# An expert layer computed transposed, with its weights copied by VectorE, in a GNN and mixture-of-experts kernel

## The chip, the cores and the metric

The kernel runs on one core of a Trainium2 chip. A core has TensorE (matmuls, its clock granted at 1.2 or 2.4 GHz), VectorE, ScalarE, GpSimd, and SyncE, which here only starts DMAs. Each runs its own program and they meet by semaphores. The metric is the device time of one execution in microseconds, as a median of runs; the lines below come from one profiled execution.

## The reference

There are 6250 nodes with 256 features and 100,000 edges. A GNN layer comes first (messages over the edges, sums per node, an update of the nodes); then each node is a token of a mixture of eight experts, each token going to its two best:

```python
x = x + gnn(layernorm(x), edges, ...)          # messages and node update
t = layernorm(x)
probs = softmax(t @ router_w.T); rw, re = top_k(probs, 2); rw = rw / rw.sum(-1)
out = t
for e in range(8):
    h = gelu(t @ w1[e] + b1[e])                # 256 -> 256
    out = out + combine[:, e:e+1] * (h @ w2[e] + b2[e])
x = x + out
```

All of the part treated here is float32.

## The kernel before, in words

The program is a row of blocks, each ended by a barrier of all engines: sorting of the edges, messages (the longest, from about 530 to 2112 us), node update, routing tables, and the expert block, in which the change lies.

The node update takes the 50 blocks of 125 nodes in 25 pairs. SyncE loads `x` for it (L1403), stores zeros into the slots of the routed token arrays (L1391) and loads the expert weights on the side (L1407), among them the biases `b1` and `b2`, each broadcast over 128 partitions. Before the first pair, two transposes by TensorE and one ScalarE copy turn `router_w` (L1537, L1491).

The routing block computes with VectorE the experts, the gates and each token's slot, and writes a table that says which expert each tile of 128 slots belongs to. SyncE sends the table to DRAM and back into one row (`tabrow`, L1647, L1649), and waits for it to land before the block ends. The engines load their registers from that row.

In the expert block tokens are first routed. `route(i)` on VectorE makes for node block t of choice k the normalized rows (L1849, `tensor_scalar`) and the slot's id and gate (L1850) in a ring `ts` of four buffers; GpSimd scatters them to `xsd[k]` by an indirect DMA (L1814). For the first choice ScalarE adds the base row, what the output starts from (L1914). All 50 first-choice blocks are routed before the experts start; the 50 of the second choice are spread over the first expert steps by `beside(m)`: four in each step below LY, two in each after.

Then 56 pairs of tiles (128 tokens each) run through a software pipeline: 28 first-choice pairs, then 28 second-choice pairs. In step m each engine does its part for pair m minus a lag; with names and lags of before:

- SyncE loads the pair (L1798, eight buffers deep) and, for first-choice pairs, the base rows (L1802). The load into a reused buffer waits for the row ids of eight pairs earlier (`slot_row`).
- TensorE, in this order: transposes the tokens of pair m (L1957), layer one of pair m-2 (L1967), layer two of pair m-6 (L1978), transposes the hidden rows of pair m-4 (L1988). A float32 matmul shows as two instructions, each with its own weight load. In layer one the tokens are the stationary operand and the expert's 256 columns, at an address from a register, stream past.
- VectorE, in this order: the routed rows; bias of layer one, pair m-2 (L1878); output of pair m-6: bias (L1887), then gate times it plus the base row (L1893) in the first half, gate alone (L1896) in the second; row ids and gates of pair m-1 (L1904, L1905).
- ScalarE: copy of the transposed tokens of pair m-1 (L1922), Gelu of pair m-3 (L1927), copy of the transposed hidden rows of pair m-5 (L1932).
- GpSimd: the scatters of the routed rows, and for pair m-7 two scatters of output rows into `out` (L1824): plain writes in the first half, accumulating in the second.

Semaphores hold these together: for instance TensorE's layer one of pair a waits until the bias of pair a-2 has freed its bank (`hb_ready`), and VectorE's output of pair a until the scatters of pair a-4 have landed (`y_out`).

Of the kernel before, what the change touches and what calls it, by code (L numbers as in the profile page):

```python
# [21 lines left out]
P = 128  # L22
N, D, E, X = 6250, 256, 100000, 8
KC = D // P
# [117 lines left out]
def gnn_moe_kernel(nc, x, src, dst, edge_w, mW1, mb1, ln_g, ln_b, mW2, mb2, uW1, ub1, uW2, ub2,  # L142
                   router_w, w1, b1, w2, b2, out):
    ctx = ExitStack()
    with ctx:
# [1149 lines left out]
        rwr = wcut(D)  # L1295
        ub1T = wcut(KC)
# [58 lines left out]
        rwT_ready = sem("rwT_ready")  # L1355
        tb_ready = sem("tb_ready")
# [11 lines left out]
        with nc.Block() as block:  # L1368
            @block.sync
            def _(sp):  # L1370
                sp.dma_start(uW1s, uW1[D:2 * D, :].rearrange("(k p) n -> p k n", p=P)).then_inc(uw_in, 16)
                sp.dma_start(uW2s, uW2.rearrange("(k p) n -> p k n", p=P)).then_inc(uw_in, 16)
                sp.dma_start(ub1T, ub1.rearrange("(k p) -> p k", p=P)).then_inc(uw_in, 16)
                sp.dma_start(rwr[0:X], router_w).then_inc(uw_in, 16)
                expert_weights = [(w1s[:, 0], w1[:, 0:P, :].rearrange("e p n -> p e n")),
                                  (w1s[:, 1], w1[:, P:2 * P, :].rearrange("e p n -> p e n")),
                                  (w2s[:, 0], w2[:, 0:P, :].rearrange("e p n -> p e n")),
                                  (w2s[:, 1], w2[:, P:2 * P, :].rearrange("e p n -> p e n")),
                                  (b1b, b1.rearrange("e n -> (e n)").partition_broadcast(P)),
                                  (b2b, b2.rearrange("e n -> (e n)").partition_broadcast(P))]  # L1380
                WAT = 2

                sp.wait_ge(padrow_set, 2)
                sp.dma_start(out[N:N + XD * P, :].rearrange("(d p) f -> p d f", p=P), padrow[:, :, 0:D]).then_inc(xpads_out, 16)
                UNITS = XC // (XD // 2)

                def empty_slots(n):

                    k, g, wide = (1, n * (XD // 2), XW) if n < UNITS else (0, (n - UNITS) * (XD // 2), XB)
                    slots = xsd[k][g * P:(g + XD // 2) * P, :].rearrange("(g p) f -> p g f", p=P)  # L1390
                    sp.dma_start(slots, padrow[:, g % XD:g % XD + XD // 2, 0:wide]).then_inc(xpads_out, 16)  # L1391

                def step(m):
                    a = m - UA
                    if a.within(NP2):
                        wait(sp, y1b_ready, a.of(1, -1))
                        sp.dma_start(un[a.mod(2)], ud[bass.ds(a.of(), 1)].rearrange("t p k u n -> (t p) k (u n)")).then_inc(un_in[a.mod(2)], 16)
                    s = m.mod(RP)
                    if m.within(NP2):
                        wait(sp, xh_ready, m.of(1, 1 - RP))  # L1400
                        rows = x[bass.ds(m.of(2 * NB), 2 * NB), :].rearrange("(u p) f -> p u f", p=NB)
                        for p in PARTS:
                            sp.dma_start(xp[s][p], rows[p]).then_inc(xp_in[s], 16)  # L1403
                        empty_slots(m.c)
                    if isinstance(m.it, int) and WAT <= m.c < WAT + len(expert_weights):
                        into, rows = expert_weights[m.c - WAT]
                        sp.dma_start(into, rows).then_inc(fw_in, 16)  # L1407
                for m in range(NP2 + UA):
                    step(Step(0, RP, m))
                for n in range(NP2, 2 * UNITS):  # L1410
                    empty_slots(n)
                sp.wait_ge(fw_in, 16 * (2 * KC + 2))
                sp.wait_ge(xpads_out, 16 * (2 * UNITS + 1))
# [74 lines left out]
            def _(act):  # L1488
                act.wait_ge(uw_in, 64)
                act.wait_ge(rw_tr, 1)  # L1490
                nc.scalar.activation(rws, ps[:, 7, 0:KC * X].rearrange("p (k e) -> p k e", k=KC), ACT.Copy).then_inc(rwT_ready, 1)  # L1491

# [40 lines left out]
            def _(pe):  # L1533
                t_ = nc.tensor
                pe.wait_ge(uw_in, 64)
                for k in range(KC):
                    last = t_.transpose(ps[:, 7, k * X:(k + 1) * X], rwr[0:X, k * P:(k + 1) * P], ident[0:X, 0:X])  # L1537
# [85 lines left out]
        with nc.Block() as block:  # L1623
# [20 lines left out]
            def _(sp):  # L1644
# [6 lines left out]
                sp.wait_ge(xtab_in, 16)  # L1651
# [92 lines left out]
        RB = 2  # L1744
        LXT, L1, LG1, L2H, LHT, L2 = 1, 2, 3, 4, 5, 6
# [10 lines left out]
        hg = cut(RH * 2 * D, "p (r u n) -> p r u n", r=RH, u=2)  # L1756
        hT = cut(RH * 2 * D, "p (r n) -> p r n", r=RH)
        hb = work[:, WORK - 2 * 2 * D:WORK].rearrange("p (r u n) -> p r u n", r=2, u=2)
# [6 lines left out]
        base_ready = sem("base_ready")  # L1765
# [4 lines left out]
        slot_row = sem("slot_row")  # L1770
        h_ps = sem("h_ps")
        hb_ready = sem("hb_ready")
        hg_ready = sem("hg_ready")
        h_tr = sem("h_tr")
# [11 lines left out]
        with nc.Block() as block:  # L1786
# [18 lines left out]
            def _(pool):  # L1805
# [3 lines left out]
                def route(i):  # L1809
                    k, t = divmod(i, BK)  # L1810
                    pool.wait_ge(ts_ready, i + 1)
                    if k == 0:
                        pool.wait_ge(base_ready, t + 1)
# [27 lines left out]
            def _(dve):  # L1841
                v = nc.vector

                def route(i):
# [4 lines left out]
                    v.tensor_scalar(ts[n_, r, 0:D], agg[n_, t, :], mv3[n_, t:t + 1, 1], mv3[n_, t:t + 1, 0], ALU.mult, ALU.add)  # L1849
# [5 lines left out]

                regs = [v.alloc_register(f"expert_of_tile{j}") for j in range(2 * (RX + L2))]
# [9 lines left out]
                for m in range(XP + L2):  # L1866
# [5 lines left out]
                    a = m - L1  # L1872
                    if 0 <= a < XP:
                        dve.wait_ge(h_ps, a + 1)
                        wait(dve, hg_ready, a - 1)
                        for u in range(2):
                            o = offs[2 * (b + L2 - L1) + u]
                            last = v.tensor_tensor(hb[:, a % 2, u], ps[:, 2 + a % 2, u * D:(u + 1) * D], b1b[:, bass.ds(o, D)], ALU.add)  # L1878
                        last.then_inc(hb_ready, 1)
                    a = m - L2  # L1880
                    if 0 <= a < XP:
# [3 lines left out]
                        for u in range(2):  # L1885
                            o = offs[2 * b + u]
                            v.tensor_tensor(yb[:, r, u], ps[:, 6 + a % 2, u * D:(u + 1) * D], b2b[:, bass.ds(o, D)], ALU.add).then_inc(y_raw, 1)  # L1887
# [11 lines left out]
                    if 0 <= a < XP:  # L1899
                        r = a % RX  # L1900
# [7 lines left out]
            def _(act):  # L1908
                act.wait_ge(ts_spare, 1)
                for t in range(BK):  # L1910
                    r = t % RS
                    if t >= RS:
                        act.wait_ge(ts_out[r], 16 * (t // RS))
                    nc.scalar.activation(ts[n_, r, XW:XB], agg[n_, t, :], ACT.Identity, bias=mv3[n_, t:t + 1, 0],  # L1914
                                         scale=xscale[n_, t:t + 1]).then_inc(base_ready, 1)

                def step(m):
                    a = m - LXT
# [5 lines left out]
                    if a.within(XP):  # L1924
                        act.wait_ge(hb_ready, a.of(1, 1))
                        wait(act, h_tr, a.of(1, 1 - RH))
                        nc.scalar.activation(hg[:, a.mod(RH)], hb[:, a.mod(2)], ACT.Gelu).then_inc(hg_ready, 1)  # L1927
                    a = m - LHT
                    if a.within(XP):
                        act.wait_ge(h_tr, a.of(1, 1))  # L1930
                        wait(act, y_ps, a.of(1, 1 - RH))
                        nc.scalar.activation(hT[:, a.mod(RH)], ps[:, 4 + a.mod(2), :], ACT.Copy).then_inc(hT_ready, 1)  # L1932
                pipeline(act, XP, L2, RX, step)

            @block.tensor
            def _(pe):
                t_ = nc.tensor
                regs = [t_.alloc_register(f"expert_of_tile{j}") for j in range(2 * (RX + L2))]
# [9 lines left out]
                def step(m):  # L1948
# [11 lines left out]
                    if a.within(XP):  # L1960
                        pe.wait_ge(xsT_ready, a.of(1, 1))
                        wait(pe, hb_ready, a.of(1, -1))
                        for u in range(2):
                            o = offs[2 * (b + L2 - L1) + u]
                            for k in range(KC):
                                c = (u * KC + k) * P
                                last = t_.matmul(ps[:, 2 + a.mod(2), u * D:(u + 1) * D], xsT[:, a.mod(RH), c:c + P], w1f[:, k, bass.ds(o, D)],  # L1967
                                                 start=(k == 0), stop=(k == KC - 1))
                        last.then_inc(h_ps, 1)
                    a = m - L2  # L1970
                    if a.within(XP):
                        pe.wait_ge(hT_ready, a.of(1, 1))
                        wait(pe, yb_ready, a.of(1, -1))
                        for u in range(2):
                            o = offs[2 * b + u]
                            for k in range(KC):
                                c = (u * KC + k) * P
                                last = t_.matmul(ps[:, 6 + a.mod(2), u * D:(u + 1) * D], hT[:, a.mod(RH), c:c + P], w2f[:, k, bass.ds(o, D)],  # L1978
                                                 start=(k == 0), stop=(k == KC - 1))
                        last.then_inc(y_ps, 1)  # L1980
                    a = m - L2H
                    if a.within(XP):
                        pe.wait_ge(hg_ready, a.of(1, 1))
                        wait(pe, hT_ready, a.of(1, -1))
                        for u in range(2):
                            for k in range(KC):
                                c = (u * KC + k) * P
                                last = t_.transpose(ps[:, 4 + a.mod(2), c:c + P], hg[:, a.mod(RH), u, k * P:(k + 1) * P], ident[:, :])  # L1988
                        last.then_inc(h_tr, 1)
# [22 lines left out]
```

## Time and profile before

| what | value |
|---|---|
| median of 3 runs | 2656.83 us (2654.34 to 2657.34) |
| the profiled execution's own time | 2656.25 us |
| its span, first to last instruction | 2654.4 us |
| mean granted TensorE clock | 0.949 of full |
| TensorE busy (matmuls) | 2380.0 us, 90% |
| VectorE busy | 2007.8 us, 76% |
| ScalarE busy | 1716.5 us, 65% |
| GpSimd busy | 1353.1 us, 51% |

The busy times are sums over stages with different limits. Times in the views are microseconds from the first instruction; the expert block runs from about 2301 us to the end, its first expert step begins at 2372.29. In a timeline row the number after the start is how long the merged instructions took from the first start to the last end, `x8` their count, and the brackets give the engine's idle time before and what ended it.

### The profile page before, as it was taken

To read this page: it belongs to the slowest core of one execution; us is meant where nothing else is said; L and a number is where in the kernel's file an instruction comes from. 1 tells how busy PE (TensorE), PEld (TensorE's weight loads), DVE (VectorE), ACT (ScalarE), POOL (GpSimd) and SP (SyncE) were. 2 spreads that over 40 slices of the span, in tenths; PEclk is the share of its full clock that TensorE was granted. 3 is DMA by queue.
4 is the path that set the end of the run, shared out by engine and by line. 5 is a ranking of instruction groups with operands and counts; after the bars stand their busy time and mean duration, and the time that the engine had idled before them with its cause. 6 is when DMAs were issued, how large, how long until landed. Compare 5 with 4: busy or idle time off the path is not lost. (4 is left out here: it accounts for less than half of the span.)

```text
span 2654.4 us, 61287 instructions
## 1 busy us (share of the span) xinstructions
PE 2380.0 (90%) x15214; PEld 2044.3 (77%) x15215; DVE 2007.8 (76%) x6154; ACT 1716.5 (65%) x5986; POOL 1353.1 (51%) x1342
## 2 busy tenths in 40 slices
PE   4399999789999999999999999999999889119997
PEld 4288887568888888888888888888888779117886
DVE  8999999477777777777777777777777656546653
ACT  1777777567777777777777777777777556233432
POOL 2067777465555555555555555555555101267666
PEclk7599999989999999999999999999999989559998
DMA  7011111243232323232322332323235299156675
GB/s 151 1 34 29 34 34 29 86 114 91 87 92 87 91 87 91 87 91 87 91 87 89 89 91 87 91 87 91 87 91 86 62 289 307 67 204 203 208 123 65
DMA packets 155377, 265.16 MB, mean 100 GB/s; under 512 B 31249, under 2 KB 99440, under 8 KB 154917
## 3 DMA queue, kind: packets, MB, share of 16 engines
q0 software_dynamic: 64656, 147.39, 21.2%
q1 hardware_dynamic: 90623, 116.59, 14.6%
q8 instruction: 46, 0.75, 0.1%
q14 instruction: 52, 0.43, 0.1%
HBM read 190.85 MB, written 73.02 MB: 99 GB/s over the span
## 5 line engine op out<-in xcount | busy, mean ns | idle before, releaser
L1056 POOL DMA_INDIRECT work<-dst_half,stage_i x848 | 811.6, 957 | 758.3 <-PE ps L1264 582.5
L1247 PE MATMUL ps<-W2c,work 128*128 128x256 f32 x3392 | 802.3, 379 | 0.0
L1247 PEld LDWEIGHTS ps<-W2c,work 128*128 128x128 f32 x3392 | 612.0, 190 | 70.7
L1082 DVE TENSOR_TENSOR agg<-agg,ps 125x256 f32 x848 | 354.2, 418 | 254.0 <-PE ps L1264 246.3
L1188 ACT ACTIVATE work<-ps 128x512 f32<-128x512 f32 x424 | 251.9, 594 | 351.5 <-PE ps L1264 351.4
L1264 PE MATMUL ps<-work 128*125 128x256 f32 x1696 | 435.2, 379 | 1.3 <-ACT work L1209 1.3
L1203 ACT ACTIVATE work<-work 128x256 f32<-128x256 f32 x848 | 341.4, 404 | 53.6 <-DVE work L1109 50.1
L1161 DVE SCALAR_TENSOR_TENSOR work<-ps,work,b2c 128x256 f32<-128x256 f32 x848 | 368.4, 476 | 0.0
L1238 PE MATMUL ps<-ablk,work 128*128 x2544 | 351.1, 275 | 16.3 <-DVE work L1130 10.4
L519 POOL DMA_INDIRECT edge_records<-stage,work x208 | 262.6, 1263 | 176.2 <-PE ps L946 113.2
L1195 ACT ACTIVATE work<-work 128x256 f32<-128x256 f32 x848 | 340.8, 406 | 0.3
L1238 PEld LDWEIGHTS ps<-ablk,work 128*128 128x128 bf16 x2544 | 250.3, 98 | 100.4 <-issue 19.2
L1264 PEld LDWEIGHTS ps<-work 128*125 128x125 f32 x1696 | 285.4, 188 | 25.8 <-ACT work L1209 1.7
L1153 DVE TENSOR_TENSOR work<-ps,work 128x512 f32<-128x512 f32 x424 | 289.7, 683 | 0.0
L1209 ACT ACTIVATE work<-work 128x512 f32<-128x512 f32 x424 | 265.0, 625 | 10.7 <-DVE work L1161 10.7
L1257 PE MATMUL ps<-ident,work 128*128 128x128 f32 x1696 | 255.3, 273 | 0.0
L1257 PEld LDWEIGHTS ps<-ident,work 128*128 128x128 f32 x1696 | 212.7, 141 | 42.6
L812 ACT ACTIVATE work<-work 125x52 f32<-125x52 bf16 x800 | 191.1, 327 | 42.7 <-DVE work L659 38.3
L946 PEld LDWEIGHTS ps<-work 125*128 125x128 f32 x1600 | 191.2, 195 | 32.8 <-issue 15.5
L946 PE MATMUL ps<-work 125*128 125x104 f32 x1600 | 195.5, 278 | 20.6 <-ACT work L812 18.8
L1824 POOL DMA_INDIRECT out<-work x112 | 141.6, 1264 | 64.6 <-DVE work L1896 22.0
L1172 DVE TENSOR_TENSOR work<-iota_f,rec 128x250 f32<-128x250 f32 x424 | 174.3, 411 | 0.0
(280 smaller groups left out, 3366.8 us busy)
## 6 DMA issues: line engine op xcount, KB each, us to landing
work<-tile_sources SPq DMA_DIRECT2D x106, 250.0 KB
first_choice_tokens<-work SPq DMA_DIRECT2D x14, 1028.0 KB
work<-dst_half,stage_i POOLq DMA_INDIRECT x848, 2.8
second_choice_tokens<-work SPq DMA_DIRECT2D x14, 516.0 KB
work<-first_choice_tokens SPq DMA_DIRECT2D x28, 258.0 KB, 3.7
work<-second_choice_tokens SPq DMA_DIRECT2D x28, 258.0 KB, 2.9
work<-first_choice_tokens SPq DMA_DIRECT2D x28, 256.0 KB, 3.4
update_node_half<-work SPq DMA_DIRECT2D x25, 250.0 KB, 2.2
```

The source lines that it names most:

```text
L946: last = t_.matmul(ps[:, 5, 0:2 * LO], hi1[e, r, c, :], lov[e, r, c].rearrange("p f n -> p (f n)"), start=(s + c == 0), stop=(s * SB + c = ...
L1056: pool.indirect_dma_start(bg[:, r, u, :], None, dstd, bass.IndirectOffsetOnAxis(ap=stage_i[:, c:c + 1], axis=0)).then_inc(gath[r], 16)
L1082: v.tensor_tensor(d, d, ps[0:NB, (7, 0)[a.mod(2)], u * D:(u + 1) * D], ALU.add).then_inc(agg_add, 1)
L1153: v.tensor_tensor(bg[:, r].rearrange("p u n -> p (u n)"), ps[:, 1 + s, :], bg[:, r].rearrange("p u n -> p (u n)"), ALU.add).then_inc(pre_s ...
L1161: last = v.scalar_tensor_tensor(out=zb[:, u], in0=ps[:, 5 + s, u * D:(u + 1) * D], scalar=rstd[:, z.mod(RQ), u:u + 1], in1=b2c[:, :], op0= ...
L1195: last = nc.scalar.activation(junk[:, u], sa[:, a.mod(RS), u], ACT.Square, accum_out=ssq[:, a.mod(RQ), u:u + 1])
L1203: last = nc.scalar.activation(sa[:, a.mod(RS), u], bg[:, a.mod(RB), u], ACT.Silu, accum_out=ssum[:, a.mod(RQ), u:u + 1])
L1209: nc.scalar.activation(msg[:, a.mod(2)], zb[:, :, :], ACT.Silu).then_inc(msg_ready, 1)
L1238: last = t_.matmul(ps[:, 1 + s, u * D:(u + 1) * D], ohT[:, m.mod(8) // TB, c:c + P], ablkf[:, bass.ds(o + k * D, D)], start=(k == 0), stop ...
L1247: last = t_.matmul(ps[:, 5 + s, u * D:(u + 1) * D], sT[:, a.mod(RT), u, k], W2c[:, k], start=(k == 0), stop=(k == KC - 1))
L1257: last = t_.transpose(ps[:, 3 + s, c:c + P], sa[:, a.mod(RS), u, k * P:(k + 1) * P], ident[:, :])
L1264: last = t_.matmul(ps[0:NB, (7, 0)[a.mod(2)], u * D:(u + 1) * D], eh[:, a.mod(RE), u], msg[:, a.mod(2), u], start=True, stop=True)
```

## The change

Layer one is computed transposed: the expert's weights become the stationary operand (128 x 128 blocks) and the transposed tokens stream past, 128 columns at a time, so that the hidden rows come out already transposed. The second set of transposes and their copy go, with `hb`, `hg` and their semaphores. The bias of layer one now lies along the partitions, so ScalarE's Gelu adds it, in four instructions of 128 columns for each pair in place of one of 512; for this `b1` is loaded as eight rows, turned by two more transposes of TensorE, and copied into `b1b` by ScalarE. VectorE copies each tile's expert weights, 512 floats in each partition, from the register's address into one of two buffers (`w1p`), in its step for pair m-1, ahead of the row ids and behind the output of pair m-4. The lags become L1 = 2, LG1 = 3, L2 = 4, LY = 5; layer two has four PSUM banks. The normalized rows of the second choice are made by ScalarE (`act_part`), at the start of its expert steps; VectorE keeps the id and gate copy. SyncE no longer waits for the table's landing in the routing block; the engines that read it wait when they first need it.

```diff
+                sp.dma_start(b1r[0:X], b1).then_inc(uw_in, 16)
-                                  (b1b, b1.rearrange("e n -> (e n)").partition_broadcast(P)),
...
-                act.wait_ge(uw_in, 64)
+                act.wait_ge(uw_in, 80)
+                nc.scalar.activation(b1b.rearrange("p (e n) -> p e n", e=X)[:, :, 0:KC],
+                                     ps[:, 7, KC * X:2 * KC * X].rearrange("p (k e) -> p e k", k=KC), ACT.Copy).then_inc(b1T_ready, 1)
...
+                for k in range(KC):
+                    last = t_.transpose(ps[:, 7, (KC + k) * X:(KC + k + 1) * X], b1r[0:X, k * P:(k + 1) * P], ident[0:X, 0:X])
...
-                sp.wait_ge(xtab_in, 16)
...
-        LXT, L1, LG1, L2H, LHT, L2 = 1, 2, 3, 4, 5, 6
+        LXT, L1, LG1, L2 = 1, 2, 3, 4
...
@@ VectorE, route(i) @@
+                    if k == 0:
+                        v.tensor_scalar(ts[n_, r, 0:D], agg[n_, t, :], mv3[n_, t:t + 1, 1], mv3[n_, t:t + 1, 0], ALU.mult, ALU.add)
...
@@ VectorE, step m: the bias of layer one is gone; behind the output of pair m - L2: @@
                     a = m - LXT
                     if 0 <= a < XP:
+                        wait(dve, h_ps, a - RW + 1)
+                        for u in range(2):
+                            o = offs[2 * (b + L2 - LXT) + u]
+                            v.tensor_copy(w1p[:, a % RW, u], w1f[:, :, bass.ds(o, D)]).then_inc(w1p_ready, 1)
...
@@ ScalarE @@
+                def act_part(i):
+                    k, t = divmod(i, BK)
+                    r = i % RS
+                    if i >= RS:
+                        act.wait_ge(ts_out[r], 16 * (i // RS))
+                    row, scale = ((ts[n_, r, XW:XB], xscale[n_, t:t + 1]), (ts[n_, r, 0:D], mv3[n_, t:t + 1, 1]))[k]
+                    nc.scalar.activation(row, agg[n_, t, :], ACT.Identity, bias=mv3[n_, t:t + 1, 0],
+                                         scale=scale).then_inc(act_row, 1)
...
+                        act.wait_ge(h_ps, a.of(1, 1))
                         wait(act, y_ps, a.of(1, 1 - RH))
+                        for u in range(2):
+                            o = offs[2 * b + u]
+                            for f in range(KC):
+                                c = (u * KC + f) * P
+                                last = nc.scalar.activation(hT[:, a.mod(RH), c:c + P], ps[:, 2 + a.mod(2), c:c + P], ACT.Gelu,
+                                                            bias=b1b[:, bass.ds(o + f, 1)])
...
@@ TensorE, step m @@
                     a = m - L1
                     if a.within(XP):
                         pe.wait_ge(xsT_ready, a.of(1, 1))
+                        wait(pe, hT_ready, a.of(1, -1))
+                        pe.wait_ge(w1p_ready, a.of(2, 2))
+                        for u in range(2):
+                            for f in range(KC):
+                                for k in range(KC):
+                                    last = t_.matmul(ps[:, 2 + a.mod(2), (u * KC + f) * P:(u * KC + f + 1) * P],
+                                                     w1p[:, a.mod(RW), u, k, f * P:(f + 1) * P], xsT[:, a.mod(RH), (u * KC + k) * P:(u * KC + k + 1) * P],
+                                                     start=(k == 0), stop=(k == KC - 1))
                         last.then_inc(h_ps, 1)
                     a = m - L2
                     if a.within(XP):
                         pe.wait_ge(hT_ready, a.of(1, 1))
-                        wait(pe, yb_ready, a.of(1, -1))
+                        wait(pe, yb_ready, a.of(1, 1 - RH))
-                    a = m - L2H
```

## Rows read from the trace of the kernel before

**Rows 1.** Windows: us; PE, PEld, DVE, ACT, POOL busy; PEclk; DMA share; GB/s.
```profile
2540.00:2590.00 50.00, 50.00 (x280) 44.69 (x280) 25.51 (x94) 20.27 (x36) 35.61 (x24) 1.00 0.79 121
```

**Rows 2.** The chain that ended last, from 2200 us: start, us, what.
```profile
2376.21 0.96 POOL second_choice_tokens L1814
...
2563.16 1.73 PE ps L1967 x8
...
2642.91 1.55 POOL out L1824
2644.77 1.55 POOL out L1824
```

**Rows 3.** Timeline of all engines, one step of the second half: start, us, instruction.
```profile
2560.40 1.89 PE L1978 MATMUL ps<-ablk,work 128*128 x8
...
2562.43 0.76 DVE L1887 TENSOR_TENSOR work<-ps,ablk 128x256 f32<-128x256 f32 x2 [0.97 <-PE ps L1978]
...
2562.56 0.60 PE L1957 MATMUL ps<-ident,work 128*128 128x128 f32 x4
...
2563.00 1.89 PE L1967 MATMUL ps<-ablk,work 128*128 x8
2563.11 0.61 DVE L1896 TENSOR_SCALAR work<-work 128x256 f32<-128x256 f32 x2
...
2563.63 0.16 DVE L1904 CAST work<-work 128x2 int32<-128x2 f32 x1
...
2564.73 1.89 PE L1978 MATMUL ps<-ablk,work 128*128 x8
```

**Rows 4.** VectorE's timeline, first-choice steps.
```profile
2386.12 0.75 DVE L1878 TENSOR_TENSOR work<-ps,ablk 128x256 f32<-128x256 f32 x2
...
2398.65 0.41 DVE L1849 TENSOR_SCALAR work<-agg,ablk 125x256 f32<-125x256 f32 x1 [1.42 <-DMA second_choice_tokens<-work,rec]
...
2409.14 0.74 DVE L1887 TENSOR_TENSOR work<-ps,ablk 128x256 f32<-128x256 f32 x2
2409.81 0.86 DVE L1893 SCALAR_TENSOR_TENSOR work<-work 128x256 f32<-128x256 f32 x2
2410.60 0.16 DVE L1904 CAST work<-work 128x2 int32<-128x2 f32 x1
```

**Rows 5.** TensorE's timeline, an early expert step after a long wait.
```profile
2387.11 3.56 PE L1967 MATMUL ps<-ablk,work 128*128 x8 [6.76 <-DVE work L1878]
```

**Rows 6.** TensorE's timeline where 125-column float matmuls run, and a gap.
```profile
489.42 1.05 PE L920 MATMUL ps<-agg,work 128*128 128x125 f32 x8
490.32 1.88 PE L927 MATMUL ps<-work,agg 128*125 128x512 f32 x4
...
500.32 1.13 PE L965 MATMUL ps<-work 128*128 128x256 f32 x4 [2.12 <-DVE work L730]
```

**Rows 7.** Groups of VectorE over the whole span: count, busy us, mean ns, idle before.
```profile
L1694 DVE COPY work<-ablk 125x400 f32<-125x400 f32 x2 | 1.0, 520 | 0.1
...
L568 DVE COPY work<-work 125x800 f32<-125x800 f32 x1 | 0.7, 650 | 0.0
```

**Rows 8.** A group of ScalarE, the same columns.
```profile
L1914 ACT ACTIVATE work<-agg,ablk 125x256 f32<-125x256 f32 x50 | 29.7, 600 | 60.2 <-DMA first_choice_tokens<-work,rec 32.1 <-POOL work L1807 28.0
```

**Rows 9.** SyncE's line 1802 (base rows): issues and landing.
```profile
DMA to landing us min/median/max: 2.7/3.4/4.6
```

**Rows 10.** SyncE's waits, 2280 to 2302 us: us in total, times, longest.
```profile
SPq L1623 <- DMA work<-tile_experts: 3.0, 1, 3.0
```

**Rows 11.** Waits, 2110 to 2172 us.
```profile
DVE work L1481 <- DMA work<-in_x: 27.9, 9, 7.9
```

**Rows 12.** DMA, 2110 to 2170 us: packets, MB, mean rate.
```profile
DMA packets 15532, 17.91 MB, mean 298 GB/s; under 512 B 1023, under 2 KB 15272, under 8 KB 15272
```

**Rows 13.** TensorE's timeline, update stage, around one gap.
```profile
2164.43 1.39 PE L1545 MATMUL ps<-ident,work 125*128 125x125 f32 x8 [1.69 <-ACT work L1509]
2165.62 3.29 PE L1560 MATMUL ps<-ablk,work 128*125 128x256 f32 x8
```

More of the change, by code:

```diff
@@ L1295, in gnn_moe_kernel @@
         rwr = wcut(D)
+        b1r = wcut(D)
         ub1T = wcut(KC)
@@ L1355, in gnn_moe_kernel @@
         rwT_ready = sem("rwT_ready")
+        b1T_ready = sem("b1T_ready")
         tb_ready = sem("tb_ready")
@@ L1411, in _ @@
                     empty_slots(n)
-                sp.wait_ge(fw_in, 16 * (2 * KC + 2))
+                sp.wait_ge(fw_in, 16 * (2 * KC + 1))
                 sp.wait_ge(xpads_out, 16 * (2 * UNITS + 1))
@@ L1534, in _ @@
                 t_ = nc.tensor
-                pe.wait_ge(uw_in, 64)
+                pe.wait_ge(uw_in, 80)
                 for k in range(KC):
-                    last = t_.transpose(ps[:, 7, k * X:(k + 1) * X], rwr[0:X, k * P:(k + 1) * P], ident[0:X, 0:X])
+                    t_.transpose(ps[:, 7, k * X:(k + 1) * X], rwr[0:X, k * P:(k + 1) * P], ident[0:X, 0:X])
+                for k in range(KC):
+                    last = t_.transpose(ps[:, 7, (KC + k) * X:(KC + k + 1) * X], b1r[0:X, k * P:(k + 1) * P], ident[0:X, 0:X])
                 last.then_inc(rw_tr, 1)
@@ L1743, in gnn_moe_kernel @@
         RX, RY, RS, RH = 8, 4, 4, 4
-        RB = 2
-        LXT, L1, LG1, L2H, LHT, L2 = 1, 2, 3, 4, 5, 6
+        RB, RW = 2, 2
+        LXT, L1, LG1, L2 = 1, 2, 3, 4
         LY = L2 + 1
@@ L1755, in gnn_moe_kernel @@
         xsT = cut(RH * 2 * D, "p (r n) -> p r n", r=RH)
-        hg = cut(RH * 2 * D, "p (r u n) -> p r u n", r=RH, u=2)
         hT = cut(RH * 2 * D, "p (r n) -> p r n", r=RH)
-        hb = work[:, WORK - 2 * 2 * D:WORK].rearrange("p (r u n) -> p r u n", r=2, u=2)
+        w1p = cut(RW * 2 * KC * D, "p (r u k n) -> p r u k n", r=RW, u=2, k=KC)
         w1f = w1s.rearrange("p k e n -> p k (e n)")
@@ L1764, in gnn_moe_kernel @@
         ts_out = [sem(f"ts_out{r}") for r in range(RS)]
-        base_ready = sem("base_ready")
+        act_row = sem("act_row")
         base_in = [sem(f"base_in{r}") for r in range(RB)]
@@ L1770, in gnn_moe_kernel @@
         slot_row = sem("slot_row")
+        w1p_ready = sem("pair_weights")
         h_ps = sem("h_ps")
-        hb_ready = sem("hb_ready")
-        hg_ready = sem("hg_ready")
-        h_tr = sem("h_tr")
         hT_ready = sem("hT_ready")
@@ L1811, in route @@
                     pool.wait_ge(ts_ready, i + 1)
-                    if k == 0:
-                        pool.wait_ge(base_ready, t + 1)
+                    pool.wait_ge(act_row, i + 1)
                     pool.indirect_dma_start(xsd[k], bass.IndirectOffsetOnAxis(ap=xposi[:, k, t:t + 1], axis=0),
@@ L1848, in route @@
                         dve.wait_ge(ts_out[r], 16 * (i // RS))
-                    v.tensor_scalar(ts[n_, r, 0:D], agg[n_, t, :], mv3[n_, t:t + 1, 1], mv3[n_, t:t + 1, 0], ALU.mult, ALU.add)
+                    if k == 0:
+                        v.tensor_scalar(ts[n_, r, 0:D], agg[n_, t, :], mv3[n_, t:t + 1, 1], mv3[n_, t:t + 1, 0], ALU.mult, ALU.add)
                     v.tensor_copy(ts[n_, r, D:XW], idgate[n_, k, t, :]).then_inc(ts_ready, 1)
@@ L1854, in _ @@
                     route(t)
+                dve.wait_ge(xtab_in, 16)
                 regs = [v.alloc_register(f"expert_of_tile{j}") for j in range(2 * (RX + L2))]
@@ L1871, in _ @@
                         route(i)
[L1872 to L1879, printed above, removed]
                     a = m - L2
@@ L1886, in _ @@
                             o = offs[2 * b + u]
-                            v.tensor_tensor(yb[:, r, u], ps[:, 6 + a % 2, u * D:(u + 1) * D], b2b[:, bass.ds(o, D)], ALU.add).then_inc(y_raw, 1)
+                            v.tensor_tensor(yb[:, r, u], ps[:, 4 + a % RH, u * D:(u + 1) * D], b2b[:, bass.ds(o, D)], ALU.add).then_inc(y_raw, 1)
                         if a < XPC:
@@ L1909, in _, with enter @@
                 act.wait_ge(ts_spare, 1)
-                for t in range(BK):
[L1911 to L1915, printed above, removed]
+                def act_part(i):
[6 more added lines that the diff above has]
+                                         scale=scale).then_inc(act_row, 1)
+                for t in range(BK):
+                    act_part(t)
+                act.wait_ge(xtab_in, 16)
+                regs = [nc.scalar.alloc_register(f"expert_of_tile{j}") for j in range(2 * (RX + LG1))]
+                offs = [None] * (2 * (RX + LG1))
+                def enter(it):
+                    for j in range(2 * LG1):
+                        nc.scalar.reg_mov(regs[j], 0 if isinstance(it, int) and it == 0 else regs[2 * RX + j])
+                    nc.scalar.load(regs[2 * LG1:], tabrow[0:1, bass.ds(it * (2 * RX) + PADT, 2 * RX)])
+                    offs[:] = [nc.scalar.snap(r, min_val=0, max_val=(X - 1) * D) for r in regs]
                 def step(m):
+                    b = m.c % RX if isinstance(m.it, int) else m.c - RX
                     a = m - LXT
@@ L1924, in step @@
                     if a.within(XP):
[L1925 to L1930, printed above, removed]
-                        wait(act, y_ps, a.of(1, 1 - RH))
-                        nc.scalar.activation(hT[:, a.mod(RH)], ps[:, 4 + a.mod(2), :], ACT.Copy).then_inc(hT_ready, 1)
-                pipeline(act, XP, L2, RX, step)
+                        act.wait_ge(h_ps, a.of(1, 1))
+                        wait(act, y_ps, a.of(1, 1 - RH))
+                        for u in range(2):
[4 more added lines that the diff above has]
+                                                            bias=b1b[:, bass.ds(o + f, 1)])
+                        last.then_inc(hT_ready, 1)
+                for m in range(XP + LG1):
+                    if m % RX == 0:
+                        enter(m // RX)
+                    for i in beside(m):
+                        act_part(i)
+                    step(Step(0, RX, m))
             @block.tensor
@@ L1937, in _ @@
                 t_ = nc.tensor
+                pe.wait_ge(xtab_in, 16)
                 regs = [t_.alloc_register(f"expert_of_tile{j}") for j in range(2 * (RX + L2))]
@@ L1961, in step @@
                         pe.wait_ge(xsT_ready, a.of(1, 1))
-                        wait(pe, hb_ready, a.of(1, -1))
+                        wait(pe, hT_ready, a.of(1, -1))
+                        pe.wait_ge(w1p_ready, a.of(2, 2))
                         for u in range(2):
[L1964 to L1968, printed above, removed]
+                            for f in range(KC):
[3 more added lines that the diff above has]
+                                                     start=(k == 0), stop=(k == KC - 1))
                         last.then_inc(h_ps, 1)
@@ L1977, in step @@
                                 c = (u * KC + k) * P
-                                last = t_.matmul(ps[:, 6 + a.mod(2), u * D:(u + 1) * D], hT[:, a.mod(RH), c:c + P], w2f[:, k, bass.ds(o, D)],
+                                last = t_.matmul(ps[:, 4 + a.mod(RH), u * D:(u + 1) * D], hT[:, a.mod(RH), c:c + P], w2f[:, k, bass.ds(o, D)],
                                                  start=(k == 0), stop=(k == KC - 1))
                         last.then_inc(y_ps, 1)
-                    a = m - L2H
[L1982 to L1989, printed above, removed]
                 pipeline(pe, XP, L2, RX, step, enter)
```

## The prediction

> **What bounds the kernel now.** I read the windows first, then the chain that ended last, then the timeline of all engines step by step. In the second half of the expert stage the windows show TensorE busy in 50.00 of 50 us at full clock, while VectorE, ScalarE and GpSimd are busy in 25.51, 20.27 and 35.61 [rows 1]. The chain runs there through L1967 and L1978, the two expert layers, and ends in GpSimd's scatters into `out` [rows 2]. So the stage is bound by TensorE, and only the last scatters by GpSimd. One step of two tiles takes 2564.73 - 2560.40 = 4.33 us [rows 3]: 1.73 for each layer [rows 2], 0.44 for the transposes of the tokens (L1957, 2562.56 to 2563.00) and 0.43 for those of the hidden rows (L1988), which is what remains. The reader is to see that no engine waits for its neighbour in a closed ring: the bias of the first layer (L1878) is made two steps ahead of where TensorE needs its bank again, the last layer follows four steps after the first.
>
> **The change, part by part.** I number TensorE's step m: it transposes tile pair m, does layer one of pair m-2 and layer two of pair m-4. What decides is the order inside VectorE's step m. It does the output of pair m-4 first (waits for layer two of TensorE's step m) and only then copies the weights of pair m-1. TensorE's step m+1 begins layer one of pair m-1 only with these copies. So layer two of step m, VectorE's output work, the copies, and layer one of step m+1 stand in one ring; nothing in it overlaps but the 0.44 us of token transposes. RW = 2 buffers don't help, since the copy is late in program order, not short of a buffer.
>
> The ring of a second-half step:
> - Layer one: 16 instructions of 128 columns in place of 8 of 256. Where TensorE runs eight with 125 columns, each with its own weight load, they start 490.32 - 489.42 = 0.90 us before the next line [rows 6], 0.1125 each: 1.80 us. The bound below is today's 1.73.
> - Layer two, and until VectorE begins the output add: 2562.43 - 2560.40 = 2.03 [rows 3].
> - Adds until the gate multiply 0.68, gate multiply until the next instruction 0.52 [rows 3].
> - Two copies of 512 floats. The nearest rows: 800 contiguous floats in 650 ns (0.81 ns each), 400 read in another order in 520 ns (1.30 ns each) [rows 7]. So one costs 0.42 or 0.67 us. I take 0.42, since these copies read runs of 256 contiguous floats; in a queue two take 0.76.
> - VectorE's end until TensorE begins: 2387.11 - (2386.12 + 0.75) = 0.24 [rows 4, 5].
> Sum 1.80 + 2.03 + 0.68 + 0.52 + 0.76 + 0.24 = 6.03 us, against 4.33 now. In the first half the output uses the base rows: 0.67 and 0.79 [rows 4] in place of 0.68 and 0.52, so 6.29. There the base load is also new in the way. SyncE issues it after the load of the tokens, which waits for the row ids that VectorE writes behind the copies. From the output adds on: 0.67 + 0.79 + 0.76, 0.2 for ids and gates (one is 0.16 [rows 3]), 0.6 for SyncE and the load ahead (my guess, no row), and 3.4 median landing [rows 9], is 6.4; the multiply that needs it comes at 6.29 + 0.67 = 6.96. The median fits, the longest (4.6) is some 0.7 late: I add 0.1 a step, 6.39.
>
> Start: VectorE's twentieth second-choice row, the last of its step 4, is started at 2398.65 after a wait for a DMA [rows 4], which the change keeps. Then a short copy, output of pair 0 (1.46), copies (0.76), 0.24: layer one of step 5 begins at about 2401.4. TensorE has then idled over 3 us, and after such a wait eight matmuls took 3.56 in place of 1.89 [rows 5]: 1.7 more. From step 5 to step 57 there are 27 rings with base rows and 25 without: 27 x 6.39 + 25 x 6.03 = 323.3, so layer one of step 57 begins at 2726.4. Its output (pair 53) is handed on at 1.80 + 2.03 + 1.2 + 0.1 later, 2731.5. GpSimd then has three pairs left, six scatters 1.86 apart [rows 2], 10.9 us: end at 2742.4. Before, it was 2644.77 + 1.55 = 2646.3. The stage adds 96.1 us.
>
> What lies beside other work: GpSimd needs 3.72 us a step in the second half, and in steps that route four issues of 0.96 + 0.31 [rows 2], 5.1: both under the ring. ScalarE: its costliest nearby instruction, 256 columns with bias and scale, is 600 ns [rows 8]; token copy, four Gelu and two second-choice rows at no more than that each are 4.2 us, and its results have a whole step of slack. Cost nothing; if switching between Identity and Gelu took it over 1 us a time it would pass 6.3. The 0.43 us of removed transposes, the removed hidden bias adds and the affine taken from VectorE lie outside the ring: worth nothing.
>
> Gains outside: the broadcast of `b1`, 128 x 8 KB = 1.05 MB, goes from a stretch in which VectorE waits 27.9 us for `x` [rows 11] and DMA moves 298 GB/s [rows 12]: 3.5 us at most, I take 3. The small load of `b1`, two more transposes and one more ScalarE copy, some 0.5, lie under that wait. The wait for the table's landing at the end of the routing stage cost SyncE, the last to arrive, 3.0 us [rows 10]; the expert stage asks for it 60 us later. Together -6.0.
>
> **The clock.** TensorE idles 6.03 - 0.44 - 1.80 - 1.73 = 2.1 us in each ring, 2.4 with base rows. After a wait of 2.12 us four matmuls took 1.13, the speed of 2.4 GHz [rows 6]. After one of 1.69 us, behind matmuls of few columns, eight took 3.29 in place of 1.89 [rows 13], the speed of 1.2 GHz. Between these I take one step in ten with 1.6 us more: 5 x 1.6 = 8. The Trainium skill (TensorE: Matmul & The Clock Gate, "A second HAM failure mode: psum-queue depth-cycling") tells of a kernel whose short idle between groups of matmuls made the clock go to and fro; the same page, "Why this matters for your kernels", sets only longer idle as harmful. By the second the sum would be without the 8 us; the first is a rival below.
>
> Sum on the profiled span: 2654.4 + 96.1 - 6.0 + 8 = 2752.5. The median lies 2.4 above the span (launch and spread): 2755 us.
>
> **Rivals.**
> - The clock goes to and fro (20%). If it falls in half the steps, 26 x 1.6 = 42 in place of 8: 2789. If it never rises, both layers double in each: 52 x 3.5 = 182, some 2930. For it: rows 13's gap was shorter than these. Against: the 2.12 us gap, and each ring has 3.5 us of dense matmuls. That page's rule on micro-idle would act here in this way.
> - The copies run at 1.30 ns a float (10%): 52 x 0.5 = 26 more, 2781. For it: the source's address comes from a register and skips between two blocks.
> - The other side (7%): the ring is not closed, because VectorE reaches the copies before TensorE's layer two ends. Then a step is 0.44 + 1.80 + 1.73 = 3.97, 52 of them 206.4 in place of 323.3, without the clock's 8: 2630. It decides from the point where the copies of pair m-1 end before layer two of step m does. For it: TensorE would then be full as now [rows 1]. Against: the program order of both engines.
> - A small loss or none (3%), should two of the ring's latencies be hidden in a way that I don't see: 2656 to 2728.
>
> **How the numbers follow.** The forecast, ring closed and clock mostly high, has 60%, with 2735 to 2775 for itself. The range takes in the slow copies and a clock that falls in up to 28 steps more (45 us) and, below, a ring 0.5 us shorter: 2728 to 2825, leaving out 10% below and 6 to 10% above. Differences under 0.2% (5 us) can't be told from none here: faster 0.07, same 0.01, slower 0.92.
>
> **What would show it.** Right: TensorE's busy share in the expert stage near two thirds; L1's matmuls waiting for VectorE's weight copy in nearly each step, 2 us and more; steps of 6.0 and 6.3 to 6.4 us; VectorE's output add waiting for layer two each time; the copies at 0.42 us; layer one 1.8 us at full clock; GpSimd's second-half scatters waiting over 2 us a step; expert stage starting 6 us earlier. Wrong: TensorE without gaps (the ring is open); copies over 0.6; granted clock well under 1.00 in the stage (the first rival); base multiplies waiting for their DMA over 0.3 us a step.

## The result and the profile after

The changed kernel takes 2762.15 us (median of 4 runs, 2760.49 to 2763.55) beside 2655.93 us of the kernel before: ratio 1.0397, interval 1.0385 to 1.041, so 4% slower. The profiled execution has a span of 2758.8 us, 104.4 above that of before. The forecast was 2755 us.

In the expert block no engine is full any more. Windows of the changed kernel (us; PE, PEld, DVE, ACT, POOL busy; clock; DMA share; GB/s), two of the first half and one of the second, where rows 1 had TensorE at 50.00:

```profile
2440.00:2490.00 50.00, 35.42 (x205) 31.93 (x206) 18.73 (x76) 19.16 (x49) 27.75 (x29) 0.90 0.46 148
...
2540.00:2590.00 50.00, 34.27 (x207) 30.36 (x205) 18.68 (x64) 13.34 (x39) 15.34 (x14) 0.93 0.36 106
...
2640.00:2690.00 50.00, 35.34 (x234) 31.06 (x232) 17.85 (x68) 15.26 (x44) 27.41 (x17) 1.00 0.56 90
```

TensorE is busy in 34 to 35 of 50 us in each, VectorE in 18 to 19. Note the clock: 0.90 and 0.93 in the first half, 1.00 in the second, with the same busy time. Who waits for whom in the block, 2395 to 2740 us (us in total, times, longest):

```profile
DVE work L1882 <- PE ps L2003: 221.1, 54, 5.5
...
PE ps L1991 <- DVE work L1898: 100.7, 53, 2.2
...
POOL out L1825 <- DVE work L1891: 60.5, 25, 4.0
```

VectorE's output add (L1882) waits for layer two (L2003) 54 times, and TensorE's layer one (L1991) for the weight copy (L1898) 53 times. Two engines that wait for each other in each step are a ring. One step of the second half, which answers to [rows 3]:

```profile
2641.36 0.76 DVE L1882 TENSOR_TENSOR work<-ps,ablk 128x256 f32<-128x256 f32 x2 [3.83 <-PE ps L2003]
...
2642.03 0.61 DVE L1891 TENSOR_SCALAR work<-work 128x256 f32<-128x256 f32 x2
2642.56 0.76 DVE L1898 COPY work<-ablk 128x512 f32 x2
...
2643.37 2.05 PE L1991 MATMUL ps<-work 128*128 128x128 f32 x16 [1.71 <-DVE work L1898]
...
2645.26 1.89 PE L2003 MATMUL ps<-ablk,work 128*128 x8
...
2646.98 0.60 PE L1981 MATMUL ps<-ident,work 128*128 128x128 f32 x4
2647.29 0.76 DVE L1882 TENSOR_TENSOR work<-ps,ablk 128x256 f32<-128x256 f32 x2 [3.83 <-PE ps L2003]
```

From add to add it is 5.93 us: add to gate multiply 0.67, to the copies 0.53, to layer one 0.81, layer one 1.89, layer two to the next add 2.03. Only the token transposes (2646.98) overlap. TensorE's timeline shows the second thing, the fall of its clock, which answers to [rows 13]; the last two lines are from the end of the block:

```profile
2432.84 3.25 PE L1991 MATMUL ps<-work 128*128 128x128 f32 x16 [1.99 <-DVE work L1898]
2435.88 2.39 PE L2003 MATMUL ps<-ablk,work 128*128 x8
...
2440.68 2.05 PE L1991 MATMUL ps<-work 128*128 128x128 f32 x16 [1.98 <-DVE work L1898]
...
2446.89 3.60 PE L1991 MATMUL ps<-work 128*128 128x128 f32 x16 [1.99 <-DVE work L1898]
2450.28 2.02 PE L2003 MATMUL ps<-ablk,work 128*128 x8
...
2454.71 2.05 PE L1991 MATMUL ps<-work 128*128 128x128 f32 x16 [1.98 <-DVE work L1898]
...
2595.91 2.05 PE L1991 MATMUL ps<-work 128*128 128x128 f32 x16 [1.71 <-DVE work L1898]
...
2601.84 2.05 PE L1991 MATMUL ps<-work 128*128 128x128 f32 x16 [1.71 <-DVE work L1898]
...
2727.07 3.62 PE L1991 MATMUL ps<-work 128*128 128x128 f32 x16 [2.24 <-DVE work L1898]
2734.67 2.02 PE L1991 MATMUL ps<-work 128*128 128x128 f32 x16 [2.25 <-DVE work L1898]
```

Layer one after an idle time of 1.98 or 1.99 us takes 3.25 or 3.60 us in some steps and 2.05 in others; in the second half, behind 1.71, always 2.05. At the end it takes 3.62 us behind 2.24 us of idle time, and in the next step 2.02 behind 2.25. Starts lie about 6.20 us apart after a plain first-half step and 7.78 to 7.85 after a slow one. The copies and the layer in the groups, 2290 to 2760 us (count, busy us, mean ns, idle before):

```profile
L1991 PE MATMUL ps<-work 128*128 128x128 f32 x896 | 133.5, 311 | 102.0 <-DVE work L1898 100.7 <-issue 1.3
...
L1898 DVE COPY work<-ablk 128x512 f32 x112 | 42.4, 422 | 0.0
```

### The profile page after: what moved, and what is told of

Its sections match the earlier page's. It is cut to its first block and busy times, and to the rows that moved or that the text cites. A ratio compares the mean times of both kernels' runs of the same rounds, so it can differ in the third digit from the quotient of the medians.

```text
span 2758.8 us, 61696 instructions
## 1 busy us (share of the span) xinstructions
PE 2388.9 (87%) x15440; PEld 2054.6 (74%) x15441; DVE 1986.2 (72%) x6104; ACT 1745.7 (63%) x6149; POOL 1365.5 (49%) x1342
## 5 line engine op out<-in xcount | busy, mean ns | idle before, releaser
L1991 PE MATMUL ps<-work 128*128 128x128 f32 x896 | 133.5, 311 | 102.0 <-DVE work L1898 100.7
L1825 POOL DMA_INDIRECT out<-work x112 | 151.7, 1355 | 138.0 <-DVE work L1891 62.8
```

## The experiments

**The copies ahead of the output.** In VectorE's step:

```diff
+                    a = m - LXT
+                    if 0 <= a < XP:
+                        wait(dve, h_ps, a - RW + 1)
+                        for u in range(2):
+                            o = offs[2 * (b + L2 - LXT) + u]
+                            v.tensor_copy(w1p[:, a % RW, u], w1f[:, :, bass.ds(o, D)]).then_inc(w1p_ready, 1)
                     a = m - L2
                     if 0 <= a < XP:
                         dve.wait_ge(y_ps, a + 1)
...
                     a = m - LXT
                     if 0 <= a < XP:
-                        wait(dve, h_ps, a - RW + 1)
-                        for u in range(2):
-                            o = offs[2 * (b + L2 - LXT) + u]
-                            v.tensor_copy(w1p[:, a % RW, u], w1f[:, :, bass.ds(o, D)]).then_inc(w1p_ready, 1)
                         r = a % RX
```

> The changed kernel with one thing moved: in VectorE's step the weight copies of pair m-1 stand ahead of the output of pair m-4. My theory (a ring of layer two, output, copies, layer one): the ring opens, a step becomes TensorE's own 0.44 + 1.8 + 1.73 = 3.97 us in place of 6.20 and 5.93, TensorE has no gaps, the clock stays up; some 52 x 2.1 + 18 = 127 us less than the changed kernel, about 2630 us, faster than the kernel before. Rival (the changed kernel is bound by the clock and by 128-column matmuls, not by the order): within 20 us of 2762.

Measured: 2658.6 us, ratio 1.0005 (0.9995 to 1.0014). Moving these four lines takes 103.5 us off the changed kernel, so the ring is shown. It is 29 us short of my number. Windows of this kernel, the waits of the block, and two layers one in a row:

```profile
2440.00:2490.00 50.00, 40.59 (x273) 36.23 (x273) 22.81 (x88) 24.47 (x67) 37.02 (x37) 1.00 0.66 205
2490.00:2540.00 50.00, 42.74 (x286) 37.62 (x284) 24.99 (x86) 17.96 (x51) 24.11 (x22) 1.00 0.52 159
2540.00:2590.00 50.00, 49.62 (x354) 46.54 (x355) 29.99 (x105) 20.86 (x61) 40.34 (x26) 1.00 0.78 134
```

```profile
DVE work L1894 <- DMA work<-first_choice_tokens: 61.8, 27, 4.0
...
PE ps L1993 <- DVE work L1880: 22.5, 21, 3.7
```

```profile
2580.00 1.95 PE L1993 MATMUL ps<-work 128*128 128x128 f32 x16
...
2583.95 1.95 PE L1993 MATMUL ps<-work 128*128 128x128 f32 x16
```

In the second half TensorE is full, with a step of 3.95 us as forecast (3.97). In the first half it is not: in the routed steps GpSimd is at 37.02 of 50 us, which are spans without the 0.3 us between its issues; with them it has no gap from 2421 to 2482 us, at some 5.1 us a step. VectorE waits 61.8 us, in 27 steps, for the base rows' load (L1894), and TensorE for VectorE. From 2482 us, with the routing done, GpSimd itself waits about 2 us a step for VectorE, so that what is left there is the base load.

**The affine back on VectorE**, with the copies first (`if k == 0` goes from `route`, `act_part` from ScalarE's steps):

> As the kernel with the copies first, and the second-choice rows' affine goes back from ScalarE to VectorE. If the affine's move matters once the ring is open (VectorE then does 1.5 output, 0.8 copies, 0.3 ids, 2 x 0.5 routed rows, 3.6 us of work in a step of 3.97 us), it is up to 10 us slower than the copies-first kernel. Rival: TensorE is the bound, the same within 3 us.

Measured: 2660.3 us, ratio 1.0011 (1.0002 to 1.002), 1.7 us above the kernel without it, in overlapping intervals. The affine's move is worth nothing that can be measured, open ring or not.

**Four weight buffers** (`RW = 4`, two of them in free space of `ablk`), nothing moved:

> The changed kernel with four buffers for the copied weights in place of two, nothing moved. My theory (the copy is late in program order): the same within 3 us. Rival (the copy waits for its buffer): VectorE copies ahead, and it comes down by tens of us toward 2640.

Measured, in one execution only: 2762.37 us, 0.2 above the changed kernel. The buffers were no limit.

**The kernel before without the wait for the table:**

```diff
-                sp.wait_ge(xtab_in, 16)
...
+                dve.wait_ge(xtab_in, 16)
+                pe.wait_ge(xtab_in, 16)
```

> The kernel before, only without SyncE's wait for the table at the end of the routing block (VectorE and TensorE wait for it when they load their registers). By the wait of 3.0 us, the expert block starts 2.6 to 3.4 us earlier and the whole is 3 us (0.1%) faster. Rival: the wait only moves to VectorE or TensorE, no change.

Measured: 2656.19 us, ratio 0.9995 (0.9986 to 1.0004), 1.1 us below the kernel before where 3 were expected, and too small for the timing. In the traces VectorE's last instruction of the routing block and the first one of the expert block start so, in the kernel before, in the changed one, and in this one:

```profile
2295.77 0.21 DVE L1725 CAST rec<-work 125x100 int32<-125x100 f32 x1
...
2301.18 1.81 POOL L1807 MEMSET work<- 32x2056 f32 x1 [27.98 <-POOLq L1623]
```

```profile
2294.97 0.21 DVE L1730 CAST rec<-work 125x100 int32<-125x100 f32 x1
...
2297.75 1.81 POOL L1809 MEMSET work<- 32x2056 f32 x1 [25.34 <-POOLq L1629]
```

```profile
2294.54 0.21 DVE L1724 CAST rec<-work 125x100 int32<-125x100 f32 x1
...
2297.66 1.81 POOL L1806 MEMSET work<- 32x2056 f32 x1 [25.69 <-POOLq L1623]
```

From the one to the other it is 5.41 us in the kernel before, 2.78 in the changed one and 3.12 without the wait: the wait is worth 2.3 to 2.6 us. The rest of the 3.4 and 3.5 us by which the expert block starts sooner lies ahead of it, and is no more than one trace differs from the next: with four weight buffers, where nothing was changed up to here, the block starts at 2299.86, 2.1 us later than in the changed kernel. No gain from the broadcast of `b1` can be seen either: between 2110 and 2172 us VectorE waits 27.7 us for `x` in the changed kernel, 27.9 in the one before [rows 11].

**The length of TensorE's idle time, shorter in the first half:**

```diff
-                            if a < XPC:
+                            if False:
                                 last = v.scalar_tensor_tensor(... in1=base[:, a % RB, u] ...)
```

> The changed kernel, with the first half's output made as in the second half: gate times it without the base row (part of the computation is left out). TensorE's idle time in a first-half step falls from 1.98 to about 1.71 us. If the clock falls by the length of that idle time, none of the ten slow steps of the first half stays: 27 x 0.27 + 10 x 1.6 = 23 us less, about 2739 us. Rival (the slow steps come from the routing, base loads or writes that fill the first half): 7 us less, about 2755, with some ten slow steps left.

**And longer in the second half** (`if True:` in the same place):

> The changed kernel, with the second half's output made by the longer operation of the first half, adding what lies in the base buffer (a wrong summand, the computation is changed). TensorE's idle time in a second-half step rises from 1.71 or 1.80 to about 1.98 us. If the clock falls by the length of that idle time, the second half gets slow steps as the first has, one in 2.6: 25 x 0.27 + 9 x 1.6 = 21 us more, about 2783 us. Rival (slow steps belong to what else runs in the first half): 7 us more, about 2769, and no slow steps.

Measured: 2741.47 us (20.7 below the changed kernel) and 2783.79 us (21.6 above it), forecast 23 and 21. TensorE's timelines, the first half of the shorter kernel, then the second half of the longer one:

```profile
2463.60 2.65 PE L1991 MATMUL ps<-work 128*128 128x128 f32 x16 [1.93 <-DVE work L1898]
...
2471.32 3.46 PE L1991 MATMUL ps<-work 128*128 128x128 f32 x16 [1.83 <-DVE work L1898]
```

```profile
2597.54 3.69 PE L1991 MATMUL ps<-work 128*128 128x128 f32 x16 [1.98 <-DVE work L1898]
...
2617.77 3.45 PE L1991 MATMUL ps<-work 128*128 128x128 f32 x16 [1.98 <-DVE work L1898]
```

With the idle time at 1.71 to 1.93 us the first half has three steps of more than 7.5 us in place of ten. I had expected none; the three stand behind 1.93, 1.83 and 1.84 us, while five others behind 1.84 or 1.86 are not slow. With the idle time at 1.98 to 2.08 us (2.51 in the last two steps) the second half has nine slow steps of 7.8 to 7.9 us in place of one, though no rows are routed and no base rows are loaded there. So the slow steps come and go with TensorE's idle time in the steps, not with what else runs. Whether the length of the idle time counts or its part of the step, these two kernels do not separate. A single long idle time does not settle it: behind 2.25 us at the end of the changed kernel the layer ran at full speed, and in the copies-first kernel, among idle times of about 1 us, once behind 2.64 too, but not behind 3.69:

```profile
2419.88 3.51 PE L1993 MATMUL ps<-work 128*128 128x128 f32 x16 [3.69 <-DVE work L1880]
...
2461.85 2.05 PE L1993 MATMUL ps<-work 128*128 128x128 f32 x16 [2.64 <-DVE work L1880]
```

**The base load a step sooner.** `LB = RX + 1` in place of `RX + 2`, on the copies-first kernel, on the same with the affine on VectorE, and on the changed kernel alone; beside them the kernel before with the affine by ScalarE as its only change. These four ran in a session in which the kernel before, too, took 2710.29 us, so only the ratios can be read.

> The copies-first kernel (2658.6 us) with the base rows' load issued one step sooner (lag LB 9 in place of 10). There VectorE waits 61.8 us for these loads in 27 first-half steps. In the routed steps GpSimd is busy without a gap at 5.1 us a step until 2482 us, so the base wait only hides that; after them steps take 4.8 us where TensorE needs 3.96. Expected: no wait for the base rows, the routed steps as before, GpSimd through the remaining 13 first-half pairs at 2.53 us each by 2517 in place of some 2531: 10 to 15 us faster than the copies-first kernel, about 2646. Rival: the scatters or GpSimd set all of the first half, no change.

> As the copies-first kernel with the sooner base load, and the second-choice rows' affine back on VectorE. If GpSimd sets the routed steps, the move to ScalarE is worth nothing here: the same within 3 us. Rival: VectorE, with 3.6 us a step, delays the routed rows or the output: 5 to 10 us slower.

> The changed kernel with only the sooner base load. My theory: the ring is closed without the base rows' load, the output multiply does not wait for it: the same within 3 us of 2762. Rival: part of the ring in the first half is that load: up to 10 us faster.

> The kernel before with one part of the change: the second-choice rows' affine by ScalarE at the start of its expert steps. TensorE is the bound from 2400 us on, GpSimd sets the first steps: within 3 us of the kernel before. Rival: VectorE's load in the routed steps delays TensorE (12.6 us of waits for the bias of layer one): 5 to 10 us faster; or ScalarE's rows come late behind its waits: 3 to 10 us slower.

Measured, as ratios to the kernel before: 0.9956 (0.9938 to 0.9973), 0.9938 (0.9921 to 0.9955), 1.0309 (1.0285 to 1.0333) and 1.0001 (0.999 to 1.0012). The affine's move gives nothing alone. With the sooner load the kernel with the affine on VectorE was 5.0 us the faster, outside the 3 us expected, though the intervals overlap. And the third didn't come out at 1.040. In that session there are stretches in which TensorE's instructions are issued one by one; in the first of these four kernels, inside layer one:

```profile
2455.92 1.34 PE L1993 MATMUL ps<-work 128*128 128x128 f32 x8
2458.40 0.27 PE L1993 MATMUL ps<-work 128*128 128x128 f32 x1 [1.15 <-issue]
2459.81 0.27 PE L1993 MATMUL ps<-work 128*128 128x128 f32 x1 [1.14 <-issue]
```

The expert block's own steps in the third were 6.20 and 5.93 us as in the changed kernel. I ran two of them again in a later session. The texts below call it another chip, but the record names the same one, number 8, for both sessions, so the disturbance can't be put down to the chip:

> The same program as the copies-first kernel with the sooner base load, on another chip: on the first one all kernels, the one before too (2710 us), lost some 50 us, with TensorE's instructions issued one by one in places. Expected here: 10 to 15 us below the copies-first kernel's 2658.6, ratio to the kernel before 0.995, and an expert block of about 346 us against its 360. Rival: the gain there came from the disturbance, ratio 1.000.

> The same program as the changed kernel with only the sooner base load, on another chip: on the first one its ratio to the kernel before was 1.031, but its steps in the trace were those of the changed kernel (6.20 and 5.93 us). If the base load is outside the ring, the ratio here is 1.040 as for the changed kernel, the expert block 461 us. Rival: the base load was part of it, ratio 1.031 again.

Measured: 2642.91 us, ratio 0.9953 (0.994 to 0.9967), with an expert block of 343 us in place of 360; and 2761.51 us, ratio 1.0402 (1.0386 to 1.0418), the changed kernel's own. The sooner load is worth 15.7 us where the ring is open (a difference between two sessions, whose kernels before differ by 0.9 us) and nothing where it is closed. Windows of the open kernel, from the middle of the first half on:

```profile
2440.00:2490.00 50.00, 46.12 (x304) 41.26 (x302) 27.79 (x98) 26.30 (x72) 38.12 (x40) 0.97 0.69 207
2490.00:2540.00 50.00, 50.00 (x357) 46.67 (x356) 30.14 (x105) 21.65 (x62) 33.41 (x26) 1.00 0.66 173
```

TensorE is full from about 2490 us, where with the later load it was so only from 2540. By the starts of layer one in the two traces, the sixteen steps from step 5 on, in which most rows are routed, take 76.0 us in place of 81.0 (expected was no change), and the twelve behind them 47.7 in place of 59.2. Here ScalarE waits 33.1 us, 26 times, for scatters before it can make the routed rows, and TensorE in some of these steps for ScalarE. Whether the affine is better off on VectorE in this kernel is open; only the disturbed session compared the two. This kernel is faster than the kernel before and the changed one, by 0.5% and 4.3%.

## Why the prediction was right, point by point

| term | forecast, us | measured, us |
|---|---|---|
| expert block starts | -6.0 | -3.4 (2301.18 to 2297.75) |
| from there to layer one of step 5 | 100.2 | 102.3 (to 2400.04) |
| slow clock at step 5 | 1.7 | 0, it came a step earlier |
| 27 rings with base rows | 172.5 | 167.8 (27 x 6.21) |
| 25 rings without | 150.8 | 149 (5.93 to 6.03 each) |
| slow clock in the rings | 8 | 17.8 (ten of 1.62 and one of 1.6) |
| layer one of step 57 to the last scatter's end | 16.0 | 16.3 |
| from there to the end of the span | 8.1 | 7.9 |

- **The ring** was right in place and size, and the move of four lines showed it. Its terms: copies and hand-over to TensorE 0.81 against 0.76 + 0.24, layer one 1.89 in the closed ring against 1.80, and 1.79 (3.95 - 1.73 - 0.43) in the open one, one copy 422 ns as taken. The 0.1 for late base rows was not there: VectorE never waits for them in the changed kernel. The median landing was 3.4 us as taken, but the longest 4.1 in place of 4.6. The rival with slow copies (0.67 us) is out.
- **The start** came out near by luck. I had let VectorE's last routed row, behind a DMA at 2398.65, set layer one of step 5. In the trace the routed rows of step 4 are done by 2394.3. What comes last is layer one of step 4 at the slow clock and layer two behind it, so the ring is closed a step sooner than I had it:

```profile
2391.82 3.76 PE L1991 MATMUL ps<-work 128*128 128x128 f32 x16 [1.32 <-issue]
```

```profile
2397.68 0.76 DVE L1882 TENSOR_TENSOR work<-ps,ablk 128x256 f32<-128x256 f32 x2 [3.39 <-PE ps L2003]
```

- **The clock** was the term mis-sized: not one step in ten but ten in 27 of the first half, and in the second only the last but one, behind 2.24 us of idle. It cost 9.8 us more than the 8 that I took. That the whole was only 6.3 us off is in part luck too, since the rings were 6.5 us shorter than forecast. I had laid the two cases of rows 6 and 13 side by side without asking what differs between 2.4 and 2.1 us of idle, though I had worked out both. Nor were they of one measure: mine came from starts, while the profile counts idle time from the end of the last transposes, some 0.17 us less (5.93 - 0.43 - 1.89 - 1.73 = 1.88 against 1.71). Measured, the idle times were 1.98 and 1.71 (1.80 without tokens to prepare), and with the first there were slow steps, with the second none.
- **The sign rival** fell, as the program order of both engines said. But its price was too good: with the ring open the kernel came to 2658.6, not 2630, since I had let TensorE's step stand for all 56 pairs. GpSimd's 5.1 us in the routed steps and the base rows' load behind the row ids come first there. I had worked out both numbers, and used neither for this rival.
- **The gains outside** were 3.4 us in place of 6.0: the wait for the table 2.3 to 2.6 us, the broadcast none that shows. Its 1.05 MB less did not shorten VectorE's wait for `x`, the wait that I had taken the 3 us from; why not is open.
- **ScalarE and the affine** cost nothing and gave nothing: 1.0001 alone, and with the ring open 1.7 us slower on VectorE in one comparison, 5.0 us faster in the disturbed one, with overlapping intervals both times.

Where did the gain of the transposed layer go? TensorE's own step fell from 4.33 to 3.95 us, some 21 us over 56 pairs. In the changed kernel the ring covers it; the best kernel is 13.5 us below the kernel before, with the table's wait in this number. That the rest lies under GpSimd in the routed steps is argued from the traces, not tested.

## What to carry to other kernels

Before costing an edit that makes one engine feed another, write each engine's program order beside the waits and look for a ring: what one engine does in a step only after the other's step, and gives to its next. Its price is the sum of all latencies in it, whatever the busy shares say, and the cure may be an exchange of two blocks of lines, not a buffer. When a ring is opened, ask at once which transfer was hidden by it; here that was the next 16 us.

## What the runs showed of the hardware

With bursts of some 4 us of matmuls and transposes, TensorE's clock stayed at 2.4 GHz through all 23 rings of the changed kernel with an idle time of 1.69 to 1.81 us, and fell to 1.2 GHz behind ten of 28 with 1.98 to 2.13 us and again behind 2.24 us near the end, at 1.6 us each time. A quarter of a microsecond of VectorE's work (the base add) so cost 0.27 us of ring and, on the mean over the first half, 0.6 us of clock. It is not each such idle time that lowers the clock: behind 2.25 us, and in the copies-first kernel once behind 2.64, the layer ran at full speed. The Trainium skill (TensorE: Matmul & The Clock Gate, "Why this matters for your kernels") puts the harm at longer idle times than these; the traces disagree. Its section "A second HAM failure mode: psum-queue depth-cycling" tells of such a to and fro in another kernel, from short idle times between groups of matmuls, as is seen here.
